# Sooner casts of x, scores with the other sign, and re-dealt splits in a three-layer decoder block

## The chip, the core and the metric

The kernel runs on one core of a Trainium2 chip. The metric is the device time of one execution in microseconds, on the slowest core (here the only one). Engines are TensorE (PE; its weight loads are PEld), VectorE (DVE), ScalarE (ACT), GpSimd (POOL) and SyncE (SP), which here only issues DMAs.

## What is computed

Three post-norm layers over 8 batches of 128 tokens by 512 features, all in float32:

```
x = layernorm(x + self_attention(x))      # 32 query heads of 16, 8 key/value heads, rotary, causal
x = layernorm(x + cross_attention(x, ctx))# rmsnorm(x)*w first; 32 heads of 128, bias + mask, softmax, w_out
x = layernorm(x + base(x) + lora_mixture(x))
self_attention: scores = rot(q) @ rot(k).T / 4, masked where key > query
                attn = exp(scores - rowmax) / sum;  out = (attn @ v) @ Wo.T
```

A float32 product is made of three products of rounded parts: each operand is split in a high part (a cast to the PE's fast float32 form, `_hi`) and a low part (the operand minus its high part, `_lo`), and `PARTS` takes hi·hi, hi·lo and lo·hi. So for each operand some engine casts and another subtracts before the PE can start.

## The kernel before

Every engine has one instruction stream, written out by hand. The streams meet at semaphores.

**Self-attention** (`self_attention`, L195) is a software pipeline over steps t = 0 to 11, each of eight positions j = 0 to 7. An engine's stream calls `step(t, j)` in that order. At step t the batch t is projected (`x_times`, L543: k and v at j = 0, q in two halves at j = 1 and 2); its q and k are turned by the rotary tables (`turn`, L430, DVE), added (`rot`, L317, POOL), split into stacks of high, high and low parts (L321 and L326 POOL; L415 ACT and L523 to L528 DVE), and transposed one step later (`stack`, L591, or `first_stack`, L575, for batch 0). Two steps later come eight score tiles of four heads, one a position (`scores`, L607). DVE adds the causal table and takes the row maximum in one pass (L450), writing `sm`; for even tiles POOL subtracts the maximum (L302) and ACT takes one exponential (L379); for odd tiles DVE negates the maximum (L456) and ACT takes four exponentials with it as bias (L384). The PE transposes the result, ACT copies it (L392), the PE multiplies with v (`pv`, L621) and with the output weights (`output`, L642), and the last step of a batch normalises it (`y` L461, roots on POOL L281, `x1` and `xn` L484 to L487, transposed at j = 4 and split at j = 5 and 6).

The input x of a batch is loaded to `xT_raw` by SP (L266, which waits until the batch before is split), cast by ACT at j = 3 of the step before it is needed (`xT_hi`, L346, called at L398) and subtracted by POOL at j = 5 (`xT_lo`, L276). The output weights are split on DVE in four pieces at step 2 (`WOUT_PIECES`, L240: pieces 0 and 1 at j = 3, one each at j = 5 and 6).

**Cross-attention** (`layer`, L719) is a loop over 16 groups of two heads, four tiles each (`step`, L1576 on the PE). Its first weights and the context are split during steps 8 and 9 of self-attention (LAST is 10): `hi_c` on POOL (L924) casts a quarter of the context, `lo_c` on DVE (L1369) subtracts it; `first_hi` and `first_lo` do the same for weights. The PE's `first_project` and `first_project_v` already run in step 9. The join of the two layers is L1392 to L1399 on DVE, L1681 to L1686 and `first_tiles` (L1438) on the PE.

**The last layer** follows the last group in one block (L1310 to L1349 on DVE, L1616 to L1656 on the PE): statistics, normalisation, transposes of x2 (`transpose_x2`), their split (`hi_x2` on ACT, `lo_x2` on DVE, L1209), the LoRA products by pairs of batches (`experts_a(p)`, L1526, which waits for the low parts of batches 2p and 2p + 1), a small softmax (`soft(p)`, L1221) and the base product (`base(b)`).

## Time and profile before

| | us |
|---|---|
| median of 3 runs (1120.22 to 1123.21) | 1120.84 |
| the profiled execution, its own time | 1118.23 |
| its span (first to last instruction) | 1116.4 |
| PE busy | 1072.6 (96% of the span) |
| DVE busy | 559.1 (50%) |
| ACT busy | 524.4 (47%) |
| POOL busy | 247.7 (22%) |
| TensorE clock granted, mean | 0.991 |

A line of a timeline gives start, duration, engine, line, operation and tiles, xcount, and in brackets how long the engine was idle before it and what ended the wait. A merged line ends when its last instruction does.

### The profile page before, as it was taken

The numbers are of one execution on the slowest core, as the hardware profiler recorded it, in microseconds if no ns is written. First come the engines' busy times: TensorE is split into PE (matmuls) and PEld (weight loads), VectorE is DVE, ScalarE is ACT, GpSimd is POOL, SyncE is SP. The second block draws the span as 40 slices with busy tenths as digits, with TensorE's granted clock in tenths as the row PEclk, the third lists the DMA queues.
The fourth block names the chain that finished last, engine by engine and source line by source line (L and its number), as shares of the span: only waits on it lengthen the run. The fifth ranks groups of instructions, "written<-read, shape, count | busy, mean of one in ns | idle before, by whom it ended". The sixth has DMA issues, their size and how long they took to land.

```text
span 1116.4 us, 19570 instructions
## 1 busy us (share of the span) xinstructions
PE 1072.6 (96%) x6522; PEld 927.3 (83%) x6522; DVE 559.1 (50%) x2026; ACT 524.4 (47%) x1445; POOL 247.7 (22%) x255
## 2 busy tenths in 40 slices
PE   5889989899999999999999999999999999999998
PEld 5767757688888888888888888888888888888876
DVE  5778899643434343434343343434343434343664
ACT  3789897353434343443444343434343534344412
POOL 6556666410101010101010101010101111010142
PEclk9899999999999999999999999999999999999989
DMA  4210101050202020202020110101010102000002
GB/s 145 87 49 16 45 2 57 11 215 9 81 0 80 0 80 0 80 0 80 0 80 25 54 49 31 61 19 61 19 61 19 61 19 75 4 23 1 1 1 76
DMA packets 17255, 49.60 MB, mean 44 GB/s; under 512 B 2496, under 2 KB 4928, under 8 KB 16832
## 3 DMA queue, kind: packets, MB, share of 16 engines
q1 hardware_dynamic: 16800, 45.97, 12.0%
q0 software_dynamic: 416, 3.15, 0.7%
q8 instruction: 19, 0.31, 0.1%
q14 instruction: 20, 0.16, 0.0%
HBM read 47.02 MB, written 2.10 MB: 44 GB/s over the span
## 4 chain that ended last, share of the span: by engine, by line
PE 84%; DVE 5%; ACT 4%; issue 4%; POOL 2%; DMA 1%; SPq 0%; POOLq 0%; ACTq 0%; DVEq 0%
PE bank L715 48%; PE bank L1505 15%; PE bank L1492 5%; PE bank L1475 5%; PE bank L1523 3%; PE bank L1482 2%; PE bank L540 2%; ACT pr L384 2%; PE bank L647 1%; PE bank L629 1%; DVE sm L450 1%; DMA stage<-in_wq 1%; PE bank L1561 1%; ACT q3T L355 1%; ACT pr L1014 0%
## 5 line engine op out<-in xcount | busy, mean ns | idle before, releaser
L894 POOL TENSOR_TENSOR bm<-mask,bias 128x512 f32<-128x512 f32 x64 | 97.2, 1519 | 713.5 <-DVE nmx L1174 458.1
L1014 ACT ACTIVATE pr<-sm,nmx 128x128 f32<-128x128 f32 x256 | 99.8, 391 | 226.9 <-DVE nmx L1174 226.7
L1186 DVE TENSOR_TENSOR at_lo<-bank,at_hi 128x512 fp32r<-128x512 f32 x64 | 44.3, 692 | 268.7 <-ACT at_hi L1028 268.7
L1192 DVE TENSOR_TENSOR acc<-acc,bank 128x512 f32<-128x512 f32 x128 | 88.0, 689 | 120.3 <-PE bank L1505 120.3
L1007 ACT COPY v<-bank 128x256 f32<-128x256 f32 x124 | 46.2, 372 | 118.0 <-PE bank L715 66.5
L1505 PE MATMUL bank<-wo_hi,at_hi 128*128 128x512 f32 x256 | 101.0, 395 | 0.3 <-DVE acc L1192 0.3
L1505 PE MATMUL bank<-wo_lo,at_hi 128*128 128x512 f32 x256 | 100.4, 392 | 0.0
L1505 PE MATMUL bank<-wo_hi,at_lo 128*128 128x512 f32 x256 | 99.7, 389 | 0.0
L715 PE MATMUL bank<-wv_hi,cT_hi 128*128 128x256 f32 x512 | 92.0, 302 | 0.0
L1001 ACT COPY kT<-bank 128x512 f32<-128x512 f32 x64 | 37.4, 585 | 98.3 <-PE bank L715 98.3
L715 PE MATMUL bank<-wv_hi,cT_lo 128*128 128x256 f32 x512 | 81.9, 282 | 0.0
L715 PE MATMUL bank<-wv_lo,cT_hi 128*128 128x256 f32 x512 | 81.9, 282 | 0.0
L715 PE MATMUL bank<-xnT_hi,wqk_hi 128*128 128x512 f32 x252 | 74.8, 418 | 0.0
L1475 PEld LDWEIGHTS bank<-kT,qT 128*128 128x128 f32 x512 | 66.8, 191 | 5.9 <-ACT kT L1001 1.1
L715 PEld LDWEIGHTS bank<-wv_hi,cT_lo 128*128 128x128 f32 x512 | 70.3, 190 | 0.0
L715 PEld LDWEIGHTS bank<-wv_lo,cT_hi 128*128 128x128 f32 x512 | 70.0, 190 | 0.0
L715 PEld LDWEIGHTS bank<-wv_hi,cT_hi 128*128 128x128 f32 x512 | 69.5, 191 | 0.2
L715 PE MATMUL bank<-xnT_lo,wqk_hi 128*128 128x512 f32 x252 | 69.2, 396 | 0.0
L715 PE MATMUL bank<-xnT_hi,wqk_lo 128*128 128x512 f32 x252 | 69.1, 396 | 0.0
L1492 PE MATMUL bank<-prT,v 128*128 128x128 f32 x512 | 68.0, 275 | 1.0 <-ACT prT L1022 0.7
L715 PE MATMUL bank<-cT_hi,wqk_hi 128*128 128x512 f32 x252 | 68.8, 394 | 0.0
L1475 PE MATMUL bank<-kT,qT 128*128 128x128 f32 x512 | 67.4, 274 | 0.7 <-ACT kT L1001 0.7
(233 smaller groups left out, 2269.9 us busy)
## 6 DMA issues: line engine op xcount, KB each, us to landing
qk_raw<-in_wqk SPq DMA_DIRECT2D x32, 512.0 KB, 4.3
o_raw<-in_wo SPq DMA_DIRECT2D x16, 512.0 KB, 3.4
v_raw<-in_wv SPq DMA_DIRECT2D x15, 512.0 KB, 4.3
xT_raw<-in_xT SPq DMA_DIRECT2D x8, 256.0 KB, 2.7
acc<-in_x POOLq DMA_DIRECT2D x1, 2048.0 KB, 9.9
bias<-in_bias SPq DMA_DIRECT2D x16, 128.0 KB, 3.1
out<-acc SPq DMA_DIRECT2D x8, 256.0 KB, 2.0
stage<-in_wq SPq DMA_DIRECT2D x2, 512.0 KB, 6.7
```

The source lines that it names most:

```text
L384: e = nc.scalar.activation(pr[:, 1, r], sm[:, 1, r], ACT.Exp, bias=nmx[:, r:r + 1], accum_out=sums1[b % 2][:, GROUPS[i], r:r + 1])
L715: ins = nc.tensor.matmul(out, lhs, rhs, start=start and i == 0, stop=i == len(pairs) - 1)
L894: nc.gpsimd.tensor_tensor(bm[:, s % 2], mask[:, HALF * (s // HG):HALF * (s // HG + 1), :], bias[:, s % HG:s % HG + 1, :].broadcast_to([P, ...
L1001: nc.scalar.copy(kT[:, m % 2], bank[:]).then_inc(s_kT, 1)
L1007: nc.scalar.copy(v[:, b, :], PX[b % 2][:, 0:HG * DH2]).then_inc(s_vc, 1)
L1014: e = nc.scalar.activation(pr[:, s % 2, k], sm[:, s % 2, k], ACT.Exp, bias=nmx[:, s % 2, k:k + 1], accum_out=sums[:, s % 2, k:k + 1])
L1186: nc.vector.tensor_tensor(at[1][:, s // HG, s % HG], PO[:], f32(at[0][:, s // HG, s % HG]), ALU.subtract).then_inc(s_al, 1)
L1192: nc.vector.tensor_tensor(acc[:, b], acc[:, b], PX[b % 2][:], ALU.add).then_inc(s_acc, 1)
L1475: ins = nc.tensor.matmul(S[s % 2][:, tok], qT[:, s % 2, tok], kT[:, s % 2, tok], start=True, stop=True)
L1492: ins = nc.tensor.matmul(PO[:, k * T:(k + 1) * T], v[:, half * HALF + k, i * DH2:(i + 1) * DH2], prT[:, k], start=True, stop=True)
L1505: ins = nc.tensor.matmul(PX[b % 2][:], at[p][:, half, i, tok], wo[q][:, i, :], start=i == 0 and (p, q) == PARTS[0], stop=i == HG - 1 and ( ...
L1523: ins = nc.tensor.matmul(out, lhs, rhs, start=i == 0, stop=stop and i == len(pairs) - 1)
```

## The change

Six edits:

1. **x.** ACT casts batch b at j = 7 of step b - 2 instead of j = 3 of step b - 1 (for b from 2). Batch 1 is loaded at once, to `on`, which is free then; the loads of the later batches so have `xT_raw` one batch sooner. POOL subtracts batch 2 at j = 1 of step 1 instead of j = 5.
2. **Sign.** The tables for q are negated, so scores come with the other sign; DVE takes the minimum, the exponentials have scale -1, and the negation L456 is gone.
3. **First stacks.** Six transposes of batch 0 go to six banks (`TA, O0, O1, SA, SB_, PT` for `TA, O0, O1, TA, O1, TA`), without waits for their copies. The k part of batch 0 is added on DVE instead of POOL (one more DVE instruction), cast at j = 4 and stacked at j = 4.
4. **Output weights.** Their low parts are made at j = 6 (one piece) and j = 7 (three pieces) of step 2.
5. **Steps 8 and 9.** Context quarters 1 and 3 are cast by ACT and subtracted by POOL; 0 and 2 by POOL and DVE as before. The subtraction of the first q and k weights moves on DVE from step 8, j = 3, to j = 7; that of the first v weights is cut in two (step 9, j = 1 and 3).
6. **Both ends of cross-attention.** At the join DVE does the reciprocals before `y`, POOL spreads them before the roots, the PE projects k before v. In the last layer DVE does `lo_x2(2)` and `lo_x2(3)` ahead of two statistics and of `soft(0)`.

```diff
-    WOUT_PIECES = {3: (0, 1), 5: (2,), 6: (3,)}
-    FIRST_STACK_BANKS = (TA, O0, O1, TA, O1, TA)
+    WOUT_PIECES = {6: (0,), 7: (1, 2, 3)}
+    FIRST_STACK_BANKS = (TA, O0, O1, SA, SB_, PT)
...
+        sp.dma_start(x_raw(1), a["xT"][1]).then_inc(s_x1_in, 16)
...
-        sp.dma_start(xT_raw[:], a["xT"][1]).then_inc(s_x, 16)
+        sp.dma_start(xT_raw[:], a["xT"][2]).then_inc(s_x, 16)
...
-        for b in range(2, B):
+        for b in range(3, B):
...
-            if j == (3 if t == 0 else 5) and live(t + 1):
+            if j == (3, 1)[t] if t < 2 else j == 5 and live(t + 1):
                 xT_lo(t + 1)
...
-                    nc.scalar.activation(pr[:, 0], sm[:, 0], ACT.Exp).then_inc(s_p, 1)
+                    nc.scalar.activation(pr[:, 0], sm[:, 0], ACT.Exp, scale=-1.0).then_inc(s_p, 1)
                 else:
-                    act.wait_ge(s_neg, n // 2 + 1)
+                    act.wait_ge(s_mn, n + 1)
...
-            if j == 3 and live(t + 1):
-                xT_hi(t + 1)
+            if j == 3 and t == 0:
+                xT_hi(1)
+            if j == 7 and live(t + 2):
+                xT_hi(t + 2)
...
-                        sm[:, j % 2, r], SA[:, r * T:(r + 1) * T], causal[:], 1.0, MASKED,
-                        ALU.add, ALU.max, mx[:, j % 2, r:r + 1])
-                ins.then_inc(s_mx, 1)
-                if j % 2 == 1:
-                    dve.wait_ge(s_mx, n + 1)
-                    nc.vector.tensor_scalar(nmx[:], mx[:, 1], -1.0, None, ALU.mult).then_inc(s_neg, 1)
+                        sm[:, j % 2, r], SA[:, r * T:(r + 1) * T], causal[:], 1.0, -MASKED,
+                        ALU.add, ALU.min, mn[:, j % 2, r:r + 1])
+                ins.then_inc(s_mn, 1)
...
-            if k == 3:
-                pe.wait_ge(s_k3T, 2)
-                pe.wait_ge(s_k3Tb, 2)
-            if k > 3:
-                pe.wait_ge(s_q3T, k - 3)
...
+            def odd_lo_c(k):
+                pool.wait_ge(s_chi[1], k // 2 + 1)
+                nc.gpsimd.tensor_tensor(piece(cT[1], k), raw_piece(k), f32(piece(cT[0], k)), ALU.subtract)\
+                    .then_inc(s_clo[1], 1)
...
+                    if j == 3 and t in (LAST - 2, LAST - 1):
+                        odd_hi_c(1 if t == LAST - 2 else 3)
...
-                    if t == LAST - 2 and j == 3:
+                    if t == LAST - 2 and j == 5:
+                        even_lo_c(0)
+                    if t == LAST - 2 and j == 7:
                         first_lo(wqk[0], qk_raw[0][:], s_wqk_h[0], s_wqk[0])
...
-            step_a(LAST, 0)
             step_a(LAST, 1)
+            step_a(LAST, 0)
...
+                    project_k(0, 1, S[1])
                     project_v(HALF + 1)
-                    project_k(0, 1, S[1])
...
                     accumulate(n, 1, 5)
+                    lo_x2(2)
+                    lo_x2(3)
                     stats_x(4)
                     stats_x(5)
+                    accumulate(n, 2, 6)
+                    accumulate(n, 3, 7)
                     soft(0)
-                    accumulate(n, 2, 6)
-                    lo_x2(2)
-                    lo_x2(3)
-                    accumulate(n, 3, 7)
```

ACT's stream around j = 7 and j = 3 of a step in the middle (steps 4 and 5). Before, from j = 3: the copy of a transposed tile, the cast of x, the copies of a q stack and of the spread reciprocals `y`.

```order
L379 ACTIVATE pr<-sm 128x512
L392 COPY stage<-bank 128x512
L349 CAST xT_hi<-xT_raw 128x512
L355 CAST q3T<-bank 128x512
L406 COPY y<-bank 128x512
```

Of the change, from j = 6 to j = 0 (the cast of k, an exponential, a copy, then the cast of x):

```order
L432 CAST k<-rot 128x8x16
L391 ACTIVATE pr<-sm 128x512
L404 COPY prT<-bank 128x512
L361 CAST xT_hi<-xT_raw 128x512
L396 ACTIVATE pr,logit<-sm,mn 128x128 x4
L404 COPY stage<-bank 128x512
L370 CAST k3T<-bank 64x4x128
```

The cast now stands between the copy of a tile and the four exponentials of the last odd tile; at j = 3 the q stack follows the copy directly.

DVE's stream in the last layer, before: the end of `soft(0)` (its product into `qk_raw`), an accumulation, the subtraction of batches 2 and 3 (`xnT_lo`), an accumulation, `norm_x` of batches 4 and 5.

```order
L1237 TENSOR_TENSOR qk_raw<-bank,alpha 128x256
L1192 TENSOR_TENSOR acc<-acc,bank 128x512
L1212 TENSOR_TENSOR xnT_lo<-bank,xnT_hi 128x4x128 x2
L1192 TENSOR_TENSOR acc<-acc,bank 128x512
L1206 TENSOR_SCALAR qk_raw<-acc,mv_x,rstd_x 128x512 x2
```

Of the change, from the `norm_x` pair of batches 2 and 3:

```order
L1244 TENSOR_SCALAR qk_raw<-acc,mv_x,rstd_x 128x512 x2
L1230 TENSOR_TENSOR acc<-acc,bank 128x512
L1250 TENSOR_TENSOR xnT_lo<-bank,xnT_hi 128x4x128 x2
L1234 BN_STATS st_x<-acc 128x6
L51 MEMSET spare 128x1
L1237 BN_AGGR mv_x<-st_x 128x2
L1234 BN_STATS st_x<-acc 128x6
L51 MEMSET spare 128x1
```

The subtraction now follows the accumulation of batch 5 at once; two statistics, the accumulation of batch 6 and all of `soft(0)` stand behind it instead of ahead.

## Rows read from the trace of the kernel before

**Rows 1.** Busy time by stretch, whole kernel cut at events named in the prediction.
```profile
core 0: us, PE busy (x) PEld busy (x) DVE busy (x) ACT busy (x) POOL busy (x), PEclk, DMA share, GB/s
...
66.57:150.95 84.38, 77.65 (x581) 63.18 (x577) 72.65 (x401) 75.99 (x227) 53.69 (x64) 1.00 0.07 24
150.95:170.81 19.86, 15.95 (x112) 11.60 (x108) 18.22 (x87) 18.68 (x58) 12.36 (x16) 1.00 0.09 28
...
262.00:1066.00 804.00, 802.68 (x4789) 706.21 (x4787) 336.29 (x1059) 331.15 (x903) 95.88 (x68) 1.00 0.11 37
1066.00:1116.40 50.40, 43.44 (x222) 35.43 (x222) 28.62 (x79) 9.60 (x18) 14.51 (x30) 0.93 0.11 42
```

**Rows 2.** Timeline of steps 0 to 2, start us, us, engine, operation [idle before].
```profile
11.26 0.62 ACT L349 CAST xT_hi<-xT_raw 128x512 fp32r<-128x512 f32 x1 [0.92 <-POOL k3T L296]
...
18.44 1.06 PE L540 MATMUL bank<-ident,k 128*128 128x128 f32 x8 [0.52 <-DVE k L528]
...
21.70 1.06 PE L540 MATMUL bank<-ident,q 128*128 128x128 f32 x8 [1.75 <-DVE k3T L510]
...
24.83 1.26 POOL L279 TENSOR_TENSOR xT_lo<-xT_raw,xT_hi 128x512 fp32r<-128x512 f32 x1
...
26.15 1.22 PE L715 MATMUL bank<-wkv_hi,xT_hi 128*128 128x256 f32 x4 [2.02 <-POOL xT_lo L279]
...
27.64 0.29 DVE L450 CUSTOM_DVE_ANT_0 sm<-bank,causal 128x128 f32<-128x128 f32 x1
```

**Rows 3.** Timeline of step 2.
```profile
37.80 1.28 DVE L514 TENSOR_TENSOR wout_lo<-acc,wout_hi 128x512 fp32r<-128x512 f32 x2
...
40.58 0.80 PE L617 MATMUL bank<-k3T,q3T 128*128 128x256 f32 x2 [1.62 <-DVE mx L450]
...
48.97 0.36 DVE L523 COPY k<-k 128x128 f32<-128x128 f32 x1
```

**Rows 4.** Timeline of steps 5 to 7: the cast of x, the wait behind it, j = 7.
```profile
102.22 0.62 ACT L349 CAST xT_hi<-xT_raw 128x512 fp32r<-128x512 f32 x1
...
105.40 0.66 PE L540 MATMUL bank<-ident,pr 128*128 128x128 f32 x4 [1.12 <-ACT pr L384]
...
109.73 0.33 SPq L266 DMA_DIRECT2D xT_raw<-in_xT  x1
...
112.15 0.40 ACT L384 ACTIVATE pr<-sm,nmx 128x128 f32<-128x128 f32 x1
...
115.31 0.58 ACT L358 CAST k3T<-bank 64x512 fp32r<-64x512 f32 x1 [1.04 <-PE bank L540]
...
147.36 0.66 PE L540 MATMUL bank<-ident,pr 128*128 128x128 f32 x4 [0.68 <-ACT pr L384]
```

**Rows 5.** Loads of x (L266), issue to landing.
```profile
DMA to landing us min/median/max: 2.4/2.7/3.4
```

**Rows 6.** Timeline of steps 8 and 9.
```profile
165.25 1.21 DVE L1376 TENSOR_TENSOR wqk_lo<-qk_raw,wqk_hi 128x1024 fp32r<-128x1024 f32 x1
...
167.37 0.50 PE L617 MATMUL bank<-k3T,q3T 128*128 128x256 f32 x2 [1.66 <-DVE mx L450]
...
175.43 1.18 PE L1429 MATMUL bank<-xnT_hi,wqk_hi 128*128 128x512 f32 x4
...
178.78 1.19 DVE L1376 TENSOR_TENSOR wv_lo<-qk_raw,wv_hi 128x1024 fp32r<-128x1024 f32 x1
...
180.97 0.47 PE L617 MATMUL bank<-k3T,q3T 128*128 128x256 f32 x2 [1.20 <-DVE mx L450]
```

**Rows 7.** The negation L456, all of its 32 instances.
```profile
L456 DVE TENSOR_SCALAR nmx<-mx x32: 170/170/1036, 31.4 to 197.4; 128x4 f32<-128x4 f32 x32
```

**Rows 8.** Timeline of the join.
```profile
203.84 0.66 PE L638 MATMUL bank<-ident,stage 128*128 128x128 f32 x4 [3.15 <-POOL stage L311]
...
204.10 1.63 DVE L487 SCALAR_TENSOR_TENSOR xn<-x,cols,lnw 128x512 f32<-128x512 f32 x1
...
206.29 1.12 PE L540 MATMUL bank<-ident,xn 128*128 128x128 f32 x4
...
220.38 1.16 PE L1475 MATMUL bank<-kT,qT 128*128 128x128 f32 x8 [0.68 <-ACT kT L1001]
```

**Rows 9.** Timeline of the last layer, where the PE stands longest.
```profile
1064.36 0.16 DVE L1225 TENSOR_TENSOR logit<-bank,logit 128x32 f32<-128x32 f32 x1
...
1067.07 1.28 DVE L1212 TENSOR_TENSOR xnT_lo<-bank,xnT_hi 128x512 fp32r<-128x512 f32 x2
...
1067.90 1.05 PE L1523 MATMUL bank<-cT_hi,xnT_hi 128*128 128x144 f32 x4 [2.23 <-DVE xnT_lo L1212]
```

**Rows 10.** Busy time and granted clock of the stretch behind that wait.
```profile
1067.90:1075.00 7.10, 7.10 (x29) 6.72 (x30) 3.24 (x11) 0.23 (x1) 2.74 (x2) 0.52 0.01 2
```

More of the change, by code:

```diff
@@ L78 @@
     s_s: Any
-    s_mx: Any
+    s_mn: Any
     s_ptc: Any
@@ L110, in __init__ @@
         self.half1, self.eps1 = left(whole, "half1", [P, 1]), left(whole, "eps1", [P, 1])
-        self.mx1, self.nmx1 = left(whole, "mx1", [P, 2, R1]), left(whole, "nmx1", [P, R1])
+        self.mn1 = left(whole, "mn1", [P, 2, R1])
         self.st, self.mv, self.cols = left(whole, "st1", [P, 6]), left(whole, "mv1", [P, 2]), left(whole, "cols1", [P, 4])
@@ L312, in step @@
                                       .broadcast_to([P, R1, G1, DH1])).then_inc(s_rs16, 1)
+            if j == 1 and live(t - 4) and t >= B + 2:
+                inverse_roots(t - 4)
             if j == (3 if t == 1 else 4) and live(t):
@@ L346, in xT_hi @@
         def xT_hi(b):
-            act.wait_ge(s_x, 16 * b + 16)
+            if b == 1:
+                act.wait_ge(s_x1_in, 16)
+            else:
+                act.wait_ge(s_x, 16 * max(b, 1))
             at_least(act, s_q, b - 1)
-            nc.scalar.copy(xT[0][:, b % 2], xT_raw[:]).then_inc(s_xhi, 1)
+            nc.scalar.copy(xT[0][:, b % 2], x_raw(b)).then_inc(s_xhi, 1)
         def stack_copy(b, m, nth):
@@ L411, in step @@
                 nc.scalar.copy(onT[0][:], on[:].rearrange("p (c t) -> p c t", c=KC)).then_inc(s_onhi, 1)
-            if j == 6 and live(t):
-                act.wait_ge(s_rot, t + 1)
+            if j == (4, 3)[t] if t < 2 else j == 6 and live(t):
+                if t == 0:
+                    act.wait_ge(s_k0, 2)
+                else:
+                    act.wait_ge(s_rot, t + 1)
                 at_least(act, s_t3, 6 * t)
@@ L475, in step @@
                 at_least(dve, s_rot, t)
-                turn(KVB, D, KV1, 2)
+                turned = turn(KVB, D, KV1, 2)
+                if t == 0:
+                    turned.then_inc(s_k0, 1)
+                    dve.wait_ge(s_k0, 1)
+                    nc.vector.tensor_tensor(rot[:, D:D + KV1], rot_a[:, D:D + KV1], rot_b[:, D:D + KV1], ALU.add)\
+                        .then_inc(s_k0, 1)
                 nc.vector.tensor_copy(v1[:, t % 4].rearrange("p j (k d) -> p j k d", d=DH1)[:, :, 0:3:2, :],
@@ L520, in step @@
                                         ALU.subtract).then_inc(s_onlo, 1)
-            if j == 7 and live(t):
+            if j == (4 if t == 0 else 7) and live(t):
                 dve.wait_ge(s_khi, t + 1)
@@ L845, in _ @@
                 .then_inc(s_qk_in[1], 16)
-            sp.wait_ge(s_clo, PIECES // 2)
+            for i in range(2):
+                sp.wait_ge(s_clo[i], 1)
             sp.dma_start(mem.cT_raw, mem.context_half(a["cT"], 1)).then_inc(s_c_in, 16)
@@ L852, in _ @@
             load_o(0)
-            sp.wait_ge(s_clo, PIECES)
+            for i in range(2):
+                sp.wait_ge(s_clo[i], 2)
             def next_group(g, between=None):
@@ L942, in _ @@
                         first_hi(wv, first_v_raw, s_v_in, s_wv_h)
-                    if t == LAST - 1 and j in (2, 4):
-                        hi_c(j // 2 + 1)
+                    if t == LAST - 1 and j == 2:
+                        even_hi_c(2)
+                    if t == LAST - 1 and j == 5:
+                        odd_lo_c(3)
                     if t == LAST - 1 and j == 4:
@@ L1055, in step @@
                         exps(0, 0, True)
-                        for b in range(HALF, HALF + 2):
-                            copy_v(b, b, None)
+                        copy_v(HALF, HALF, None)
                         copy_k(1, 1, S[1])
+                        copy_v(HALF + 1, HALF + 1, None)
                         continue
@@ L1134, in step, with odd_hi_c @@
                         last_norm(b)
+            def odd_hi_c(k):
+                act.wait_ge(s_c_in if k >= PIECES // 2 else prev_a.s_stage, 16)
+                act.wait_ge(prev_a.s_q, B)
+                nc.scalar.copy(piece(cT[0], k), raw_piece(k)).then_inc(s_chi[1], 1)
             def copy_two_v(b):
@@ L1759 @@
         "ident": np.eye(P, dtype=np.float32),
-        "causal": np.where(tri, np.float32(0), np.float32(MASKED)),
+        "causal": np.where(tri, np.float32(0), np.float32(-MASKED)),
         "rope": rope_tables(),
```

78 lines of the change are left out of this document (48 added, 30 removed).

## The prediction

> **What bounds the kernel now.** I read the busy time of the engines by stretch first, then timelines of the stretches in which the PE is not full, then single groups. The stretches show where time can be won at all [rows 1]. From 262 to 1066 us the PE is busy 802.68 of 804.00 us: nothing that another engine does sooner can shorten that, and the change touches no instruction of it. What is left of the PE's idle time lies ahead of 262 and behind 1066. In steps 4 to 7 of self-attention (66.57 to 150.95) the PE is busy 77.65 of 84.38 us, with ACT at 75.99 and DVE at 72.65: three engines nearly full, so a wait there ends with whichever is late at that position. In step 8 (150.95 to 170.81) ACT is busy 18.68 and DVE 18.22 of 19.86 us, and the PE only 15.95. In the last 50.40 us the PE is idle 7 us, and the granted clock is 0.93 instead of 1.00.
>
> **Start (edits 1 and 3).** Step 0 is a chain: projection, turning, splits, transposes of the stacks, their copies. The stacks of k start at 18.44, after a wait of 0.52 for DVE's part of k; the q stacks at 21.70 stand 1.75 for DVE's copy out of the bank that they reuse; and batch 2's projection at 26.15 stands 2.02 for POOL's `xT_lo` (24.83, 1.26 long) [rows 2]. The cast of batch 1 at 11.26 waits for POOL's fills, not for x, so its load going first gains nothing. With k added on DVE and cast at j = 4, I put the k stacks at 17.95. Six stacks without a wait between them, 1.06 for two [rows 2], end at about 20.6 instead of 23.7. Batch 2's x is cast long before, its subtraction is at j = 1, so the 2.02 goes. What is late next is DVE's chain: turning q of batch 1, its low parts. I carry it through with the durations of before and get the first mask tile at 23.7 instead of 27.64, and the second scores, which stand behind the projections, about 4.9 sooner. Taken: 4.0 for the tile, plus 1.2 for the PE's work that is out of the way by then, **5.2**. Lower bound 3.0 (only the 1.75 and half of the 2.02 go, with 0.3 of the k wait), upper 6.0.
>
> **Step 2 (edit 4).** The pieces of the output weights are 0.64 each (1.28 for two), and the scores at 40.58 stand 1.62 for DVE's reduction behind two of them [rows 3]. They leave j = 3 and 5. But three now stand at j = 7 ahead of the copies of k at 48.97, 1.9 us against about 1.6 won by then, and k is the head of the next step's stacks. Net **-0.3**, between -1.5 (all three on the path) and +1.5 (the wait at 40.58 gone for good). POOL's cast of those weights stays.
>
> **Cast of x out of j = 3 (edit 1).** In step 5 ACT casts x at 102.22 for 0.62, and the PE then stands 1.12 at 105.40 for an exponential; in step 7, which has no cast of x, the wait at that position is 0.68 [rows 4]. ACT is the late engine from j = 3 to 5, so the cast's time comes back nearly whole, where the pair of waits alone says 0.44. I take 0.5 in each of steps 3 to 6, **2.0** (bounds 1.0 and 2.5, four times 0.62). At j = 7 the cast costs 0.62 between the copy and the exponentials of 112.15, and ACT idles 1.04 ahead of `k3T` at 115.31 [rows 4]: that covers it. If the cover were gone, 0.6 a step would be lost and the edit worth nothing. The load is issued on SP when POOL is done with the batch before, at 109.73 [rows 4]; it lands 2.4 to 3.4 us later [rows 5], at 112.1 or 113.1, and ACT reaches j = 7's cast at about 112.0. So ACT may stand for it up to 1.1 behind which the exponentials are queued; with the median 2.7 the stall is 0.4, still inside the 1.04 but with little over. SP's next load waits on POOL alone, as before.
>
> **Sign (edit 2).** The negation takes 170 ns, 1036 at the worst, 32 times [rows 7]. It stands on DVE, which is 86% busy in steps 4 to 7 [rows 1], and ahead of ACT's exponentials, but ACT comes to them late in these steps, so its 16 x 0.17 hides behind ACT. I give it nothing of its own, and read its slow instances in the next part. The sign in the tables, the scale in the exponential and the minimum cost what their counterparts did (below: the rival that says otherwise).
>
> **Steps 8 and 9 (edit 5).** The subtraction of the first q and k weights, 1.21 at 165.25, makes the scores at 167.37 stand 1.66; that of v, 1.19 at 178.78, makes 180.97 stand 1.20 [rows 6]. The first is moved to j = 7, where the PE's first projection at 175.43 [rows 6] needs it: that moves to about 176.7, filled by score work in part. The second is halved and costs 0.6 at each place. DVE loses two subtractions of a quarter context. ACT, which has 1.18 us free in step 8 [rows 1], gets a quarter to cast, twice the 0.62 of half its size less one start-up, about 1.1 us, in each of steps 8 and 9. So DVE's waits, 2.86 in all, turn into ACT's 1.1 twice and a late weight; net **+0.25**, between -1.5 (ACT's two casts in full, weight late, nothing hidden) and +1.5 (half of DVE's waits). POOL's subtractions, twice 1.26 for a quarter [rows 2], have DVE's old place; SP's loads of the second weights and the second half of the context wait for them and for j = 7, near 177, and are used only in the next stretch.
>
> **Join (edit 6).** The transposes at 203.84 stand 3.15 for POOL's copy; DVE's `xn` at 204.10, 1.63 long, lets those of `xn` begin at 206.29 [rows 8]. With the reciprocals first, the 3.15 shrinks, but the PE then stands for `xn`, which itself is at most 0.7 sooner. The transposes of `xn` take 1.12 for four where four take 0.66 [rows 4, 8], so the clock is at its lower level there and I expect it to be so again: 0.1 here. The k projection ahead of v takes the 0.68 wait for `kT` at 220.38 [rows 8]: 0.7. Together **0.8** (0.7 to 2.5; the upper if the clock holds for those four groups).
>
> **Last layer (edit 6).** DVE begins `soft(0)` at 1064.36 and the low parts of batches 2 and 3 only at 1067.07; `experts_a(1)` starts at 1067.90, 2.23 late [rows 9]. In the 7.10 us behind that wait the granted clock is 0.52, the lower level [rows 10]. Ahead of `soft(0)` and the statistics, the low parts are ready before 1065.7. So 2.23 goes, and if the clock had been at its higher level, 7.10 x 0.48 = 3.4 more: 5.6. Against that, batches 4 and 5 are pushed back on DVE and `experts_a(2)` comes about 0.5 late. **5.2** (2.2, the wait alone, to 5.6).
>
> **The sum.** 5.2 - 0.3 + 2.0 + 0.25 + 0.8 + 5.2 = 13.15. The profiled execution took 1118.23, 1.8 above its span and 2.6 below the median of the runs; the changed one should take 1105.1, and the median 1120.84 - 13.2 = 1107.6.
>
> **The rivals.**
> *The clock falls in the tail anyway.* The wait at 1067.90 is replaced by another, on the `hi_x2` copies or bank turns, and the stretch runs at 0.52 as before. For it: the tail's chain through DVE is dense, and the clock of the 50.40 us is 0.93 with only one long wait. Against it: the PE had been busy for 800 us until then. Gain 13.2 - 3.4 = 9.8: 1111.1. Chance 0.17.
>
> *POOL's new subtractions hold DVE.* The negation of 128x4 numbers takes 170 ns as a rule and up to 1036 [rows 7], 0.87 more for the same work; DVE operations evidently can be held while something else runs. POOL gets two subtractions of some 2.5 us in steps 8 and 9, with DVE busy 92% there [rows 1]. If each holds DVE for most of its length, 2 x 2.2 = 4.4 are lost: gain 8.8, 1112.0. Against it: these subtractions stand on POOL in every step already (`xT_lo`) and the median of the 32 negations is still 170 [rows 7]. Chance 0.12. The Trainium skill, page "SBUF — State Buffer", section "🔬 SBUF: two separate sides", says that VectorE and GpSimd share a port pair as "an exclusive lock, not a bandwidth split", held for a whole instruction, for operations such as a two-input VectorE one against a GpSimd one that reads SBUF. By that rule this rival is the forecast, and moving subtractions from DVE to POOL is the wrong direction; the row on the negation agrees with the rule in that it has slow instances.
>
> *More than I count.* The clock also holds at the join, and the relieved DVE in steps 8 and 9 gives 1.5: 3 more, 1104.4. Chance 0.12.
>
> *The minimum is slower than the maximum.* One mechanism for slower: the reduction of each score tile with its table runs 256 times in steps 2 to 9, 0.29 us each [rows 2]. DVE is free 11.73 us in steps 4 to 7 [rows 1], which hold 128 of them: 92 ns each. Gains of 13.2 over 256 are another 52. If the minimum form takes over 144 ns more, the kernel gets slower; if it takes double, (290 - 92) x 256 = 51 us less 13 of gains: 1158. Nothing in the profile speaks for it, and the operation has the same shape. Chance 0.02.
>
> *The cast at j = 7 is in the way.* If x lands late and the 1.04 does not cover it, 0.6 in four steps: 1110. Inside the range; it belongs to the forecast's 0.54.
>
> **How the numbers follow.** Forecast 1107.6 with 0.54, the rivals 0.17, 0.12, 0.12 and 0.02, and 0.03 for a change that doesn't do what it says: its waits move and none goes, because the same engines do the same work. The bounds of the terms, taken together but not all at once, give 1104 to 1111; the three rivals near it stretch that to 1102.5 and 1113.5. About 0.3%, 3.4 us, is what a measurement of this kernel can tell from no change. Within it: 0.03, that last case. Slower 0.02, faster 0.95.
>
> **What would show it.** Right: first mask tile at 23 to 25 and six stacks with no wait; in steps 3 to 6 the PE's wait at j = 4 below 0.7 and ACT's idle ahead of `k3T` below 0.6; no 1.66 in step 8; the wait of 3.15 replaced by one for `xn` of 2 to 3 us; `experts_a(1)` without a wait, at a clock near 1.00. Wrong: that clock at 0.5; `k3T` copied later in its step than before, with the PE standing for it; long DVE instructions beside POOL's two new subtractions; a reduction above 0.29 us.

## The result: 1103.84 us, and where it came from

| | before | changed |
|---|---|---|
| median of 4 runs, us | 1120.53 (1117.88 to 1123.21) | 1103.84 (1103.26 to 1104.48) |
| the profiled execution, its own time | 1118.23 | 1103.35 |
| its span | 1116.4 | 1101.5 |
| mean granted clock | 0.991 | 0.995 |

The ratio is 0.9851, with a 95% interval of 0.9827 to 0.9876: 16.7 us faster by the medians, 14.9 by the two profiled executions. The forecast was 1107.6 (1102.5 to 1113.5). The page of the changed kernel's profile gives the busy times:

```profile
span 1101.5 us, 19544 instructions
PE 1064.9 (97%) x6522; PEld 922.7 (84%) x6522; DVE 547.4 (50%) x1994; ACT 524.9 (48%) x1447; POOL 249.9 (23%) x255
```

The PE is the best ruler, since it does the same products in nearly the same order in both. How much sooner the same product starts in the changed kernel is its lead there; where the lead grows or shrinks, time was won or lost.

| event on the PE | before | changed | lead | won since the row above | forecast for that part |
|---|---|---|---|---|---|
| step 2, scores of j = 4 | 36.70 | 32.31 | 4.39 | +4.39 | +5.2 (start) |
| step 3, scores of j = 3 | 56.46 | 54.47 | 1.99 | -2.40 | -0.3 (weights' pieces) |
| step 8, scores of j = 0 | 154.52 | 150.44 | 4.08 | +2.09 | +2.0 (cast of x) |
| step 9, scores of j = 7 | 194.73 | 190.32 | 4.41 | +0.33 | +0.25 |
| first `kT,qT` tile | 210.28 | 203.29 | 6.99 | +2.58 | +0.1 |
| third `kT,qT` tile | 232.13 | 225.12 | 7.01 | +0.02 | +0.7 (k before v) |
| last (64th) `kT,qT` tile | 1047.13 | 1037.78 | 9.35 | +2.34 | 0 |
| end of the span | 1116.4 | 1101.5 | 14.9 | +5.55 | +5.2 (last layer) |

Three parts came out as computed, the start nearly, and three did not: the weights' pieces cost 2.4 and not 0.3, the join brought 2.6, and 2.3 us were won in the loop over the groups, which the change does not touch.

A row of a timeline reads as in [rows 2]. A row of a stretch reads as in [rows 1]: the stretch, its length, the busy time and number of instructions of PE, PEld, DVE, ACT and POOL, the granted clock, the DMA share and GB/s. The changed kernel's start (steps 0 to 2), to be held against [rows 2]:

```profile
19.11 1.91 PE L559 MATMUL bank<-ident,q 128*128 128x128 f32 x16
21.31 0.64 PE L733 MATMUL bank<-wkv_hi,xT_hi 128*128 128x256 f32 x4
...
22.12 0.75 DVE L542 COPY k<-k 128x128 f32<-128x128 f32 x1 [0.99 <-ACT k L432]
...
23.10 1.30 DVE L547 COPY k<-k 128x384 f32<-128x384 f32 x1
...
24.46 0.66 PE L559 MATMUL bank<-ident,k 128*128 128x128 f32 x4 [1.56 <-DVE k L547]
25.52 0.47 PE L633 MATMUL bank<-k3T,q3T 128*128 128x256 f32 x2 [0.40 <-DVE mn L467]
```

The q stacks run on end, and the projection behind them does not wait: the 1.75 and the 2.02 are gone. A new wait of 1.56 for DVE's k part of batch 1 is what is late next; I had followed DVE's chain and not seen it. The first mask tile starts at 24.44, not 23.7.

Step 2 and the beginning of step 3, timeline and the stretch behind the wait:

```profile
40.03 0.74 PE L733 MATMUL bank<-wkv_hi,xT_hi 128*128 128x256 f32 x4 [1.82 <-POOL xT_lo L285]
...
42.00 0.28 DVE L467 CUSTOM_DVE_ANT_0 sm<-bank,causal 128x128 f32<-128x128 f32 x1 [3.15 <-ACT pr L391]
...
42.84 1.89 DVE L533 TENSOR_TENSOR wout_lo<-acc,wout_hi 128x512 fp32r<-128x512 f32 x3
...
45.52 1.12 PE L559 MATMUL bank<-ident,k 128*128 128x128 f32 x4 [1.54 <-DVE k L547]
```
```profile
45.52:51.74 6.22, 5.80 (x26) 5.43 (x27) 3.78 (x25) 2.41 (x5) 2.72 (x4) 0.50 0.83 306
```

DVE stands idle 3.15 us and then does three pieces (1.89) ahead of the k that the PE waits for, 1.54. Behind the wait the granted clock is 0.50, the lower of the two levels, for 6.2 us. Before, this stretch had no such wait. A second wait has grown: for POOL's `xT_lo`, 0.73 in the kernel before, 1.82 here (the row of 40.03). The lead falls by 0.5 across it, from 6.44 to 5.93.

The cast of x in step 5, on ACT, and the PE's wait at the fifth position:

```profile
101.84 0.66 PE L559 MATMUL bank<-ident,pr 128*128 128x128 f32 x4 [0.91 <-ACT pr L396]
...
108.85 0.62 ACT L361 CAST xT_hi<-xT_raw 128x512 fp32r<-128x512 f32 x1 [0.40 <-DMA xT_raw<-in_xT]
...
111.73 0.58 ACT L370 CAST k3T<-bank 64x512 fp32r<-64x512 f32 x1 [0.23 <-PE bank L559]
```

The PE's wait, 1.12 with the cast [rows 4], is 0.91, and not below 0.7 as forecast. It brings 0.2 of the 0.5 a step. The other 0.3 is won one position earlier: the lead is 3.06, 3.34 and 3.56 at the scores of j = 4, 5 and 6 of step 5. ACT waits 0.40 for x, as worked out (2.7 us of landing against an arrival at 112.0), and the 1.04 us ahead of `k3T` [rows 4] have shrunk to 0.23. The cover held, with little left.

Steps 8 and 9 (timeline, and the stretch behind the wait):

```profile
160.88 1.06 ACT L1170 CAST cT_hi<-stage 128x1024 fp32r<-128x1024 f32 x1
162.16 2.36 POOL L953 TENSOR_TENSOR cT_lo<-stage,cT_hi 128x1024 fp32r<-128x1024 f32 x1
163.53 0.66 PE L559 MATMUL bank<-ident,pr 128*128 128x128 f32 x4 [1.86 <-ACT pr L396]
163.65 0.29 DVE L467 CUSTOM_DVE_ANT_0 sm<-bank,causal 128x128 f32<-128x128 f32 x1
```
```profile
165.01:168.34 3.33, 3.33 (x16) 1.40 (x14) 3.33 (x13) 3.33 (x12) 0.01 (x1) 0.52 0.00 0
```

The old wait of 1.66 for DVE [rows 6] is gone and a wait of 1.86 for ACT stands in its place, with the lower clock behind it. DVE's reduction beside POOL's subtraction takes its 0.29 [rows 2].

The join and the last layer:

```profile
196.95 0.62 PE L645 MATMUL bank<-prT,v 128*32 128x512 f32 x2 [0.24 <-ACT stage L404]
199.99 0.66 PE L559 MATMUL bank<-ident,xn 128*128 128x128 f32 x4 [1.98 <-DVE xn L506]
219.88 1.16 PE L1538 MATMUL bank<-prT,v 128*128 128x128 f32 x8 [1.22 <-DVE xnT_lo L517]
1056.19 0.56 PE L1569 MATMUL bank<-cT_hi,xnT_hi 128*128 128x144 f32 x4
```
```profile
199.99:204.10 4.11, 4.11 (x24) 3.57 (x25) 3.58 (x4) 1.70 (x3) 2.88 (x2) 1.00 0.00 0
1056.19:1061.67 5.48, 5.48 (x38) 4.89 (x37) 4.87 (x18) 0.23 (x1) 2.03 (x3) 1.00 0.00 0
```

In the join 3.15 [rows 8] has become 0.24 + 1.98, and the transposes of `xn` take 0.66 and not 1.12: the clock did not fall. `experts_a(1)` starts at 1056.19 without a wait, and the stretch that took 8.8 us from 1067.90 to 1076.68 [rows 9, 10] takes 5.48 at full clock.

### The profile page after: what moved, and what is told of

Its sections match the earlier page's. It is cut to its first block, busy times and chain, and to the rows that moved or that the text cites. A ratio compares the mean times of both kernels' runs of the same rounds, so it can differ in the third digit from the quotient of the medians.

```text
span 1101.5 us, 19544 instructions
## 1 busy us (share of the span) xinstructions
PE 1064.9 (97%) x6522; PEld 922.7 (84%) x6522; DVE 547.4 (50%) x1994; ACT 524.9 (48%) x1447; POOL 249.9 (23%) x255
## 3 DMA queue, kind: packets, MB, share of 16 engines
q0 software_dynamic: 416, 3.15, 0.7%
## 4 chain that ended last, share of the span: by engine, by line
PE 79%; DVE 1%; ACT 1%; issue 1%; POOL 0%; POOLq 0%; ACTq 0%
PE bank L733 46%; PE bank L1551 16%; PE bank L1538 5%; PE bank L1521 5%; PE bank L1569 3%; PE bank L1528 2%; PE bank L1607 1%; ACT pr L1045 0%; PE bank L1563 0%; PE bank L1618 0%; PE bank L663 0%; DVE sm L1207 0%; DVE xn L506 0%; POOL cols L291 0%; ACT pr L396 0%
## 5 line engine op out<-in xcount | busy, mean ns | idle before, releaser
L467 DVE CUSTOM_DVE_ANT_0 sm<-bank,causal 128x128 f32<-128x128 f32 x256 | 58.9, 286 | 18.8 <-issue 7.6
```

Source lines behind the costliest of these rows:

```text
L467: ins = nc.vector.tensor_tensor_reduce(sm[:, j % 2, r], SA[:, r * T:(r + 1) * T], causal[:], 1.0, -MASKED, ALU.add, ALU.min, mn[:, j % 2, ...
```

## The experiments

Every version is timed beside runs of the kernel before on its own chip. The names are those of the blocks below. Leads are read as above, with the changed kernel's profiled execution as the reference.

### The last layer's order

`u_tail` puts `lo_x2(2)`, `lo_x2(3)` back behind `stats_x`, `soft(0)` and `accumulate(n, 2, 6)`; `b_tail` makes the new order alone in the kernel before.

> The changed kernel with the last layer's order as before. Theory: moving the low parts of batches 2 and 3 ahead of two statistics and soft(0) is worth the wait of 2.2 us and the stretch at the lower clock, together 5.6; so the span grows from 1101.5 to about 1107.1, with a wait of some 2.2 us ahead of experts_a(1) and a granted clock of about 0.52 in the 7 us behind it. Rival: the clock falls in that stretch for another reason and only the wait was won: span about 1103.7, clock no different from the changed kernel's. The loop over the groups, which took 13.40 us a tile before and 13.36 in the changed kernel: if that difference belongs to the kernel's code, 13.36 here or a value of its own; if it belongs to the execution, either.

> The kernel before with the new order of the last layer alone. Theory: the edit stands by itself and is worth 5.5 as it is on the changed kernel: ratio to before 0.995, time about 1116.5 where before has 1122.0; no wait ahead of experts_a(1). Rival: the two ends of the kernel are coupled by something (the clock, the loads of the next layer's tables), and it brings under 4. The groups' tile: 13.41 if this is a property of the kernel before, 13.37 if it belonged to one execution or chip.

`u_tail` took 1109.54 us, ratio to before 0.9889 (0.9873 to 0.9906), against 0.9851 of the changed kernel; `b_tail` 1115.88 us, 0.9948 (0.9931 to 0.9965). The start of `u_tail` was 2.2 us late for a reason of its own (below); from the last `kT,qT` tile to the end `u_tail` loses 7.8 - 2.27 = 5.5 us. The timeline of `u_tail`:

```profile
1060.81 0.91 PE L1569 MATMUL bank<-cT_hi,xnT_hi 128*128 128x144 f32 x4 [2.20 <-DVE xnT_lo L1250]
1061.52 1.05 PE L1569 MATMUL bank<-cT_lo,xnT_hi 128*128 128x144 f32 x4
```

The wait is back, and each four products take 1.05 again where the changed kernel takes 0.61. The edit is worth 5.5 in both kernels (`b_tail` by the same reckoning 5.6): 2.2 by the wait and 3.3 by the clock. The rival with a clock that falls anyway is out.

### The cast of x

```
-            if j == 3 and t == 0:
-                xT_hi(1)
-            if j == 7 and live(t + 2):
+            if j == 3 and t != 1 and live(t + 1):
+                xT_hi(t + 1)
+            if j == 7 and t == 0:
                 xT_hi(t + 2)
```

> The changed kernel with the cast of x at j = 3 of the step before it is needed, as before, from batch 3 on. Theory: the cast stood on ACT's path there and costs 0.5 us in each of steps 3 to 6; span plus 2.0, 1103.5, and the PE's wait at the fifth position longer by 0.4 in these steps. Rival: the 2.0 us that the lead grows between the third step and the eighth come from the negation that is gone (32 x 0.17 us on DVE), and the span stays at 1101.5 within 0.5.

1107.28 us, ratio 0.9872 (0.9855 to 0.9888). The lead against the changed kernel is -0.74, -1.23, -1.74, -2.26 and -2.74 at the scores of j = 4 of steps 3, 4, 5, 6 and 7: 0.5 in each of the four steps, 2.0 in all, and the PE's waits for the exponential are 1.13, 1.13, 1.12, 1.12, as before. The theory's 0.5 a step holds; its 0.4 on that wait does not (0.2, from 0.91), the rest stands one position earlier. That the span, 1103.3, is the one expected is luck: the start is 2.1 late, 1.3 of it comes back by step 3, and 0.9 is won from step 8 to the join, none of it by this edit. By the medians the version is 3.4 slower than the changed kernel, by the ratios to before 2.4.

### The output weights' pieces

`u_wout` has the places of before, `n_wout` new ones:

```
-    WOUT_PIECES = {6: (0,), 7: (1, 2, 3)}
+    WOUT_PIECES = {3: (0, 1), 5: (2,), 6: (3,)}
```
```
-    WOUT_PIECES = {6: (0,), 7: (1, 2, 3)}
+    WOUT_PIECES = {6: (0, 1, 2), 7: (3,)}
```

> The changed kernel with the output weights' pieces at j = 3, 3, 5 and 6 of step 2 as before. In the changed kernel the lead over before falls from 6.4 us at the seventh tile of step 2 to 2.0 at the fourth of step 3. Theory: the three pieces at j = 7 make k late (a wait of 1.54) and the wait lets the clock fall (about 2 us more), so putting them back costs the 1.6 at j = 5 that the move had won, and gives 3.5 to 4.4 back: span 1099 to 1100, no wait over 1 us ahead of the k transposes of step 2, clock 1.00 from 45 to 52. Rival: the lead is lost because step 3 is bound by something that was not moved (the rotated tables, POOL), so the pieces' place makes no difference there, and the span is 1103.

> The changed kernel with three of the pieces at j = 6 and one at j = 7. DVE idles 3.15 us between j = 6 and j = 7 of step 2 in the changed kernel. Theory: two pieces of 0.64 more fit in that hole, k is ready 1.3 us sooner, the wait of 1.54 nearly goes, and with it the low clock: 3 to 4 us off, span about 1098, also 1 to 2 below the version with the pieces as before. Rival: the three pieces stand beside POOL's subtraction of x and take 0.9 to 1.8 each instead of 0.64, so the gain is under 1 us: span 1101.

`u_wout`: 1103.58 us, 0.9839 (0.9823 to 0.9856). By its profile it loses 1.2 at j = 5 of step 2 (a wait of 1.77 for DVE) and wins 4.1 from j = 0 to j = 3 of step 3 (lead -2.45 to +1.69), so the old places are 3.0 better up to there. It gave 1.6 back at the join, where its clock fell after a wait of 2.01. The span was 1100.7 where 1099 to 1100 was expected, and by the medians it is no faster than the changed kernel. `n_wout`: 1100.41 us, 0.9809 (0.9793 to 0.9826), faster than the changed kernel. Its lead goes from -1.86 to +1.55, 3.4 us. The timeline of `n_wout` at the same place, and the clock:

```profile
39.79 4.04 DVE L533 TENSOR_TENSOR wout_lo<-acc,wout_hi 128x512 fp32r<-128x512 f32 x3
...
46.30 0.65 PE L559 MATMUL bank<-ident,k 128*128 128x128 f32 x4 [0.46 <-DVE k L547]
```
```profile
43.85:50.37 6.52, 4.49 (x36) 3.84 (x35) 5.82 (x38) 5.58 (x16) 4.31 (x5) 1.00 0.49 163
```

Both sides were right in part: the three pieces take 4.04 beside POOL's work, as the rival had it, but they fit in the time in which DVE had nothing else, the wait is 0.46, and the clock stays at 1.00. With k in time the same stretch is 3.4 better, though the wait for `xT_lo` is the same (1.80): the late k and the clock behind it explain the changed kernel's loss of 2.4 and more, and without them this term would have been about +1.0.

### The sign, and 32 bytes

`u_sign` restores the maximum, the negation, the scale and the small tile `nmx1`.

> The changed kernel with the sign as before: the maximum, the negation of it after every odd tile on DVE, exponentials with scale 1, and the small tile nmx (16 bytes a partition) back in SBUF. Theory: the negation hides behind ACT in the middle steps but keeps DVE late in steps 8 and 9 and at the join, so it costs about 1 us, all of it there. A second reading: the loop over the groups took 13.41 us a tile in the kernel before and 13.37 in the changed kernel and in four versions of it; what these share against before in that stretch is the SBUF place of the weights and products, 16 bytes lower without nmx. If that is the cause, this version's tile takes 13.41, which is 2.3 us over the loop: span about 1104.8 in all. Rival for the second: it is something else of the code or the chip, and the tile stays at 13.37, span about 1102.5.

1110.39 us, ratio 0.9892 (0.9865 to 0.992), with the last layer's order the dearest of the parts I took back. From the scores of j = 4 in step 8 to the first `kT,qT` tile the lead falls from -1.80 to -5.97. Its timeline at the join:

```profile
204.66 1.12 PE L562 MATMUL bank<-ident,xn 128*128 128x128 f32 x4 [2.54 <-DVE xn L509]
205.43 2.05 PE L736 MATMUL bank<-xnT_hi,wqk_hi 128*128 128x512 f32 x4
```

DVE is late again, `xn` is late, the wait is 2.54 and the clock falls. Of the 4.2 us, 2.2 are lost before the join (the lead is -4.04 at the last scores of step 9). The timeline ahead of these shows what the negation meets:

```profile
189.83 2.35 POOL L956 TENSOR_TENSOR cT_lo<-stage,cT_hi 128x1024 fp32r<-128x1024 f32 x1
189.85 2.37 DVE L473 TENSOR_SCALAR nmx<-mn 128x4 f32<-128x4 f32 x1
```

A negation that takes 0.17 as a rule takes 2.37 beside POOL's new subtraction of edit 5, and 1.03, 0.74 and 1.04 at three other places of steps 8 and 9 (in the kernel before none took over 1.04); the lead falls from -2.81 to -4.04 behind the longest. So the rival on POOL's subtractions is right for the negation, and edit 5 stands as well as it does because edit 2 took the negation away.

And the loop is slower throughout: 13.408 us a tile. That was the second reading, and it needed a test of its own, since a longer program might do it too. `p_shift` changes no instruction:

```
         self.mn1 = left(whole, "mn1", [P, 2, R1])
+        left(whole, "unused", [P, R1])
```

> The changed kernel with an unused tile of 16 bytes a partition where nmx was; not one instruction differs. It takes 32 bytes, so that everything allocated behind it (the products' and output weights' tiles at, wo, kT, v) begins at an odd multiple of 32 bytes, as before, instead of a multiple of 64. Theory: this place alone makes the groups' tile 13.41 us instead of 13.37; plus 2.4 us over the 60 tiles, nothing elsewhere. Rival: the 13.41 of the version with the old sign come from its instructions (the negation is not in that loop, but the program is longer), and the tile stays at 13.37.

1105.86 us, ratio 0.9865 (0.9849 to 0.9881). The same 56 tiles (4th to 60th) in the stretches of before, of the changed kernel and of `p_shift`, in that order:

```profile
245.54:996.38 750.84, 750.77 (x4481) 661.67 (x4480) 306.67 (x964) 311.09 (x844) 85.09 (x56) 1.00 0.12 40
```
```profile
238.50:987.14 748.64, 748.57 (x4482) 660.33 (x4481) 306.35 (x964) 310.71 (x844) 85.10 (x56) 1.00 0.12 40
```
```profile
238.51:989.35 750.84, 750.77 (x4481) 661.91 (x4480) 306.36 (x964) 310.98 (x844) 84.99 (x56) 1.00 0.12 40
```

750.84, 748.64, 750.84: the place in SBUF alone makes 2.20 us over 56 tiles. In the program the small tile takes 32 bytes, and without it the addresses of `at`, `wo`, `kT`, `v` and `qT`, and of the mask, bias and raw-weight tiles among them, are multiples of 64 instead of odd multiples of 32. The eight other versions with the changed kernel's layout (all of this section but the three named next and `n_align`) have 13.368 or 13.369 a tile, and those with the layout of before (`b_tail`, `u_sign`, `p_shift`) 13.408.

The gain is not only where the PE reads a moved tile. In the view by groups of instructions, over the same stretches, take one product of `xnT` and `wqk`, whose tiles have the same addresses in both versions (changed kernel, then `p_shift`; busy us and mean ns stand behind the first bar):

```profile
L733 PE MATMUL bank<-xnT_hi,wqk_hi 128*128 128x512 f32 x224 | 65.5, 414 | 0.0
L734 PE MATMUL bank<-xnT_hi,wqk_hi 128*128 128x512 f32 x224 | 66.2, 418 | 0.0
```

Counted from start to start, this product holds 0.0125 of the 0.039 us a tile, those of `cT` and `wv`, which did not move either, 0.010, those of `at` and `wo` 0.013 and that of `v` 0.004. So more than half is gained on products whose own operands stayed where they were.

Could the other half of SBUF give as much? `n_align` is `n_wout` with 32 unused bytes at the right end, which moves `cT`, `wqk`, `wv` and the raw weights to multiples of 64:

> The changed kernel with three pieces of the output weights at j = 6 and one at j = 7, as in the version that took 1100.4, and an unused tile of 32 bytes at the other end of SBUF, which moves the tiles cT, wqk, wv and the raw weights from odd multiples of 32 bytes to multiples of 64. Theory: what brought 0.04 us a tile for at and wo brings something for these too: the products with wqk and wv are 60% of a tile's time, so up to 0.06 a tile, 3.6 us: time 1097. Rival: only matmuls whose moving operand is one of the shifted tiles gain, and these products' moving operands that shift (cT, wqk) are not short of anything: tile 13.37, time 1100.4 within 0.5.

1099.92 us, 0.9807 (0.9791 to 0.9823), no different from `n_wout` in time, and 13.375 a tile, 0.007 more. The theory fell: what counts is the place of something on the left side, and which tile, and for which engine's accesses, was not tried.

### The join

```
-            step_a(LAST, 1)
             step_a(LAST, 0)
+            step_a(LAST, 1)
```
and on POOL the roots ahead of the spread again.

> The changed kernel with the join's order as before (DVE: y ahead of the reciprocals; POOL: roots ahead of the spread), the order of the k and v projections kept. Theory: the wait for POOL's spread comes back to about 3.1 us and lets the clock fall, where the changed kernel waits 2.2 in two pieces at full clock: cost 2.6 less the part that comes from a DVE that is on time, so plus 1.5 to 2.5, span 1103 to 1104. Rival: what the join won was DVE's work that is gone ahead of it (the negation and the quarters), not the order: plus 0.4 at most, span 1101.9.

1103.87 us, 0.9834 (0.9808 to 0.9861). The lead is -1.25 in step 8 and -1.22 at the first `kT,qT` tile, and the median is that of the changed kernel (1103.84): the order is worth nothing. The timeline shows why:

```profile
199.27 0.66 PE L652 MATMUL bank<-ident,stage 128*128 128x128 f32 x4 [1.65 <-POOL stage L317]
201.21 0.66 PE L557 MATMUL bank<-ident,xn 128*128 128x128 f32 x4 [0.30 <-DVE xn L504]
```

1.65 + 0.30 stand where the changed kernel has 0.24 + 1.98: the PE waits for `xn` in any case. What the join won, 2.6, came from a DVE that is on time (the rival's reading; in `u_sign` 1.9 of it is gone), and from a clock that did not fall. The k projection ahead of v was not tried alone; in the trace it removes the 0.68 [rows 8], and the next wait, for `xnT_lo` at 219.88, is 1.22 where it was 0.30: the lead is 6.99 ahead of it and 7.01 behind.

### The start

`u_start` has the old banks and their waits, and `xT_lo` of batch 2 at j = 5.

> The changed kernel with three banks for the first six stacks and their waits, and with the low parts of batch 2 at j = 5 of step 1, both as before; the sooner sum and cast of the first k stay. Theory: these two are nearly all of the start's gain: the PE waits 1.7 for DVE's copy out of the bank and 2 for xT_lo again, and the second scores of step 2 start 3.5 to 4 us later than in the changed kernel; some 3.5 us on the span (1105), less what the clock gives. Rival: the first k on DVE is what brought the 4 us, and the two cost under 1.5.

1107.23 us, 0.9879 (0.9862 to 0.9896). Its timeline:

```profile
21.67 1.06 PE L559 MATMUL bank<-ident,q 128*128 128x128 f32 x8 [1.56 <-DVE k3T L529]
26.08 1.22 PE L738 MATMUL bank<-wkv_hi,xT_hi 128*128 128x256 f32 x4 [2.21 <-POOL xT_lo L285]
```

Both waits are back, and the second scores of step 2 start 3.7 us later. By this pair these two parts carry the start; the k on DVE, which was not tried alone, would have the rest of 4.4, 0.7. But the scores of j = 4 in step 2, at 32.31 in the changed kernel's profile, start 0.2 to 2.2 us later in seven versions that don't differ from it up to there, and 2.1 later in `u_cast`, which is 1.9 late ahead of the first cast that it changes. In five of these eight the second scores are already 0.8 to 2.1 late, and why stays open (in `u_tail` ACT's cast of the q weights starts at 8.68, after their load, against 8.11, but in `n_quarter` it does so at 8.54 without harm). In `n_quarter` and `u_join` the wait of 1.56 at 24.4 is the same, and the products behind it run at the lower clock:

```profile
24.35 0.66 PE L559 MATMUL bank<-ident,k 128*128 128x128 f32 x4 [1.56 <-DVE k L547]
25.73 0.92 PE L733 MATMUL bank<-wq_hi,xT_hi 128*128 128x256 f32 x4
26.44 1.05 PE L733 MATMUL bank<-wq_lo,xT_hi 128*128 128x256 f32 x4
```

(`n_quarter`; these products take 0.64 in the changed kernel.) In `b_tail`, which does not differ from the kernel before there, they start 0.8 later than in it. One pair of profiled executions tells the start's gain to within 2 us, no better, and the split among its parts no better either.

### Steps 8 and 9 dealt again

`n_quarter` moves ACT's cast of the second quarter from j = 3 to 6 and POOL's subtraction from 5 to 7.

> The changed kernel with ACT's cast of the second quarter of the context in step 8 at j = 6 instead of j = 3, and POOL's subtraction of it at j = 7 instead of j = 5. In the changed kernel that cast (1.06 us) stands ahead of four exponentials and the PE waits 1.86 at 163.53, with the clock at its lower level behind it; at j = 6 ACT idles 0.55 twice. Theory: the wait falls to about 0.8 and the clock stays up: 1.0 to 2.3 us off, span 1099.5. Rival: the PE waits there for DVE or the q stack and not for the cast (the lead only moves to another wait), or the first projection in step 9 then waits for the quarter's low part, 2.4 us on POOL: span 1101 to 1103.

1105.37 us, 0.9854 (0.982 to 0.9887), no gain. The wait of 1.86 falls to 0.91 and the lead grows by 2.2 up to j = 7, then the first projection stands 2.41 for `wqk_lo`. The rows of `n_quarter`:

```profile
171.38 2.72 DVE L1421 TENSOR_TENSOR wqk_lo<-qk_raw,wqk_hi 128x1024 fp32r<-128x1024 f32 x1
```
```profile
170.65 2.37 POOL L953 TENSOR_TENSOR cT_lo<-stage,cT_hi 128x1024 fp32r<-128x1024 f32 x1
174.25 1.16 PE L1476 MATMUL bank<-xnT_hi,wqk_hi 128*128 128x512 f32 x4 [2.41 <-DVE wqk_lo L1421]
```

The DVE subtraction, 1.21 when alone [rows 6], takes 2.72: it starts at 171.38, POOL's ends at 173.02, and 1.08 are left from there to its end at 174.10. This is the rival on POOL's subtractions, in another place where it holds. The Trainium skill ("SBUF — State Buffer", section "🔬 SBUF: two separate sides") has it so: VectorE operations with two SBUF inputs and GpSimd ones that read SBUF exclude each other for a whole instruction. The reductions have one operand in a bank, and the changed kernel's trace agrees that they are not held: 0.29 beside the same POOL instruction. `n_pool` places by that rule: DVE's two-operand work at j = 5 and 6, POOL's subtraction at j = 7 beside reductions only, no cast on ACT in step 8.

> The version with three pieces of the output weights at j = 6 (1100.4), and step 8 dealt anew: POOL casts the second quarter of the context at j = 4 and subtracts it at j = 7 (ACT's cast at j = 3 is gone), DVE subtracts the first q and k weights at j = 5 and the first quarter at j = 6. The placing follows what the runs showed: a DVE subtraction of two SBUF operands beside a POOL one took 2.72 us instead of 1.22, a reduction of a score tile from its bank beside the same POOL instruction took its usual time; so POOL's 2.4 us now stand beside reductions only. Theory: ACT's 1.06 us leave the path (the wait ahead of the exponentials' transposes at j = 5 falls by 1.0) and the first projection finds its weights: 1.0 to 1.5 less than 1100.4, 1099. Rival: DVE's subtraction at j = 6 meets POOL's cast of the v weights and is held, the last masked tile of the step is late, and nothing or less is left: 1100.4 to 1102.

1100.72 us over 6 runs, 0.9831 (0.9803 to 0.9859), as `n_wout`. Against `n_wout` it wins 0.9 at j = 5 and loses 0.8 at j = 0 of step 9 by the wait below; at j = 1, where `n_wout` waits 0.61 for `wqk_lo`, that comes back. 0.7 is left, less than the runs can tell:

```profile
166.78 1.68 DVE L1411 TENSOR_TENSOR cT_lo<-stage,cT_hi 128x1024 fp32r<-128x1024 f32 x1
167.32 2.03 POOL L958 CAST wv_hi<-qk_raw 128x1024 fp32r<-128x1024 f32 x1
169.46 0.48 PE L633 MATMUL bank<-k3T,q3T 128*128 128x256 f32 x2 [0.62 <-DVE mn L467]
```

Now POOL's cast is the one held, 2.03 for 1.04, and DVE's last tile late by 0.6, as the rival said.

## Why the prediction was right, and where its steps were not

- **What bounds.** Right: all that could be won in the loop by any engine's work was nothing. Wrong in one word: "nothing that another engine does sooner can shorten that" left out the matmuls' own time. The 0 for the loop was 2.34, shown by `p_shift`. It belongs to edit 2, where a removed 16-byte tile moves what is allocated behind it.
- **Start, 5.2.** 4.4 in the pair of profiles, inside the bounds, but no version with the same start is as early; with the latest of them only 2.2 would be left, below the lower bound of 3.0. What the term lacks is the PE's wait for k of batch 1, 1.56. DVE's copies of k, 0.22 to 0.27 and 0.36 from step 2 on, took 0.75 and 1.30 there, beside POOL's cast and subtraction of q. But the kernel before has slow instructions at this place too,

```profile
24.62 0.33 DVE L523 COPY k<-k 128x128 f32<-128x128 f32 x1 [3.07 <-ACT k L415]
24.87 1.37 DVE L524 TENSOR_TENSOR k<-rot,k 128x128 f32<-128x128 f32 x1
26.28 1.33 DVE L528 COPY k<-k 128x384 f32<-128x384 f32 x1
```

  and its first mask tile at 27.64 follows the second copy as that of the changed kernel, at 24.44, does. Its three instructions of k take longer in sum than the changed kernel's, so "the durations of before" are not what failed. The chain ended 0.7 later than I put it, and which link I had too short stays open.
- **Step 2, -0.3.** The wrong term: -2.4, below its lower bound of -1.5. "1.9 us against about 1.6 won by then" was near (the wait is 1.54, which is the lower bound's reading, all three on the path); what I left out is the clock behind the wait, which I had counted in the last layer and nowhere else.
- **Cast of x, 2.0.** Right to 0.1, in the whole, per step, and in the stall of 0.4 for the load. The place was half right: the wait named for it gives 0.2 of each 0.5.
- **Sign, 0.** Wrong in the largest way: taking it back costs 6.5 us by the medians (1110.39 against 1103.84), 4.6 by the ratios to before; by the profile 2.3 in the loop and 4.2 from step 8 to the join. "Hides behind ACT" was right for steps 4 to 7 (0.2 at one position, given back at the next) and was carried to steps where DVE is the late engine and a POOL subtraction can hold the negation for 2.37.
- **Steps 8 and 9, 0.25.** Measured 0.33, and the trade is the one described (DVE's waits gave way to one for ACT's cast, 1.86, and one for a late weight, 0.35), but the number is luck. It holds 2.4 that belong to the sign edit (the lead of `u_sign` falls from -1.61 to -4.04 in these steps) and a loss of 1.1 to the clock behind the wait of 1.86, which `n_wout` does not have; neither is in the sum. By this pair, with the negation left in, edit 5 would have lost about 2.1, more than its lower bound of 1.5. DVE's reductions were not held by POOL, its negation was.
- **Join, 0.8.** 2.6, just over its upper bound, by another way: the order brought nothing, DVE's relief and the clock did. The 0.7 for k before v was eaten by the next wait, which I had not named.
- **Last layer, 5.2.** 5.5 to 5.6 in three pairs of profiles, by the wait and the clock as computed.

The errors, -0.8 (start), -2.1, +0.1, +0.1, +1.8, +2.3 (loop) and +0.3, leave 1.8 us between 13.15 and 14.9. That they are so few is luck: 2.9 us lost that were not foreseen stand against 4.1 won that were not (join and loop). Of the rivals, "More than I count", 1104.4, is nearest to the result; its first half came (the clock held at the join), its second did not (1.5 in steps 8 and 9, measured 0.33), and 2.3 came from the loop, which the sum had at 0. As for the runs, the median moved 16.7 because the profiled execution of before was 2.3 below its median and that of the changed kernel 0.5.

## What to carry to other kernels

An edit that deletes a small buffer moves every buffer allocated behind it: compare a stretch that the edit doesn't touch, per tile, before giving the edit its gain. Where one wait on the PE costs the clock, price every wait of that length the same way, those the edit makes as well as those it removes; and ask of each removed instruction not whether it hides on average, but whether its engine is the late one in each stage. Place DVE operations whose operands all lie in SBUF where POOL is idle, and POOL's own beside DVE work that reads a bank: here two-operand subtractions were held, and so were copies of k and a negation of four numbers a partition.

## What the runs showed of the hardware

- With the left tiles behind the removed one at multiples of 64 bytes instead of odd multiples of 32, a 13.4 us tile was 0.039 us (0.3%) shorter, in nine versions against four; moving the right-hand tiles by 32 bytes as well made it 0.007 longer. More than half of the gain is on products whose own operands did not move. Which tile is responsible, and how, is open.
- After the same wait in step 8, 1.85 to 1.87 us for the same work, the granted clock was 0.52 in the changed kernel and 1.00 in `n_wout`; the stretch behind it took 1.1 us more in the one than in the other. After about 2.0 in the join it fell in `u_wout` (0.65) and not in the changed kernel, after 1.56 at the start in `n_quarter` and not in the changed kernel; after 2.2 in the last layer it fell both times (before, `u_tail`), and after 2.41 in step 9 of `n_quarter` it did not (granted clock 1.00 in the 4 us behind it). So the length of a wait alone did not tell, and each such wait is a risk of 1 to 3 us.

```profile
163.48:167.19 3.71, 3.55 (x24) 2.09 (x22) 3.63 (x13) 3.71 (x14) 0.27 (x1) 1.00 0.00 0
```

That is `n_wout`, columns as above, to be held against the row of 165.01 to 168.34.

- A DVE instruction and a POOL one that exclude each other cost whichever comes second the rest of the first, about: 2.72 for 1.22 on DVE (`n_quarter`), 2.03 for 1.04 on POOL (`n_pool`), and 2.37 for 0.17 on DVE's negation of 128x4 numbers (`u_sign`).
